# Feed-forward of a routed language-model layer: rows turned three blocks ahead in place of two, with four pairs of buffers for their halves

## What is computed

```python
h = tok(x)                                  # position, nesting and segment tables, einsum with W
h = h + attn(layernorm(h))                  # 8 heads of 64, causal mask, softmax
h = h + ffn(layernorm(h))                   # 8 experts, the best 2 of them per token

# ffn
topk_val, topk_idx = top_k(x @ router_w.T + router_b, 2)
cw = one_hot(topk_idx) * softmax(topk_val)          # weight of each expert
h1, h2 = split(x @ fc1_w[e].T + fc1_b[e], 2)        # 128 -> 2 * 256
y = (silu(h1) * h2) @ fc2_w[e].T + fc2_b[e]         # 256 -> 128
out = sum_e y * cw[e]
```

## Time and profile before

| | |
|---|---|
| time, median of 3 runs | 1257.07 us (1255.15 to 1257.45) |
| the profiled execution's own time | 1256.33 us |
| its span, first to last instruction | 1254.6 us |
| PE busy in the span | 1172.8 us (93%) |
| DVE, ACT, POOL busy | 993.3, 992.7, 755.2 us |
| feed-forward in the span | about 844 us to the end |

### The profile page before, as it was taken

One profiled execution on the slowest core, in us unless ns is written; L12 is line 12 of the kernel. 1 busy time (PEld: TensorE's weight loads), 2 busy tenths in 40 slices (PEclk: granted clock), 3 DMA queues, 4 the chain that ended last, 5 costly groups with the idle time before them and its releaser, 6 DMA issues. The chain is left out here.

```text
span 1254.6 us, 45360 instructions
## 1 busy us (share of the span) xinstructions
PE 1172.8 (93%) x13125; PEld 1031.4 (82%) x13126; DVE 993.3 (79%) x3799; ACT 992.7 (79%) x3491; POOL 755.2 (60%) x1082
## 2 busy tenths in 40 slices
PE   6899999999999999999999999729999997999996
PEld 4578888888888888888888887619999996999995
DVE  6568988888888888888888887756777774777774
ACT  2799999999999999999999998726666664666663
POOL 6436755565565555565565555544777774777775
PEclk9899999999999999999999999968999998999998
DMA  5151110100100111110010111115666663555552
GB/s 177 60 186 56 39 35 32 43 32 32 47 32 32 43 36 32 42 37 32 32 43 32 36 43 40 53 53 170 197 206 199 203 191 130 159 143 143 159 153 68
DMA packets 68049, 108.97 MB, mean 87 GB/s; under 512 B 12756, under 2 KB 32948, under 8 KB 67860
## 3 DMA queue, kind: packets, MB, share of 16 engines
q1 hardware_dynamic: 50068, 62.67, 17.7%
q0 software_dynamic: 17920, 45.55, 10.0%
HBM read 45.66 MB, written 54.11 MB: 80 GB/s over the span
## 5 line engine op out<-in xcount | busy, mean ns | idle before, releaser
L764 ACT ACTIVATE probs<-ps,neg_max 128x128 f32<-128x128 f32 (+1 forms) x1024 | 337.8, 363 | 2.0 <-DVE neg_max L961 1.9
L764 ACT ACTIVATION_READ_ACCUMULATOR probs<-ps,neg_max 128x1 f32 x1024 | 236.3, 231 | 0.0
L574 POOL TENSOR_TENSOR probs<-probs,inv_sums 128x384 f32<-128x384 f32 x120 | 99.2, 826 | 205.4 <-DVE inv_sums L910 205.4
L1143 DVE SCALAR_TENSOR_TENSOR probsT<-ps,b_now,masked 128x256 f32<-128x256 f32 x286 | 125.3, 480 | 85.5 <-PE ps L1237 66.0
L1235 PE MATMUL ps<-xT_hi,w_now 128*128 128x256 f32 x572 | 173.1, 303 | 0.8 <-DVE xT_lo L1127 0.8
L720 ACT ACTIVATE masked<-ps,b_now 128x256 f32<-128x256 f32 x286 | 119.8, 471 | 59.5 <-PE ps L1237 59.1
L1237 PE MATMUL ps<-xT_hi,w_now 128*128 128x256 f32 x572 | 162.8, 285 | 0.0
L1236 PE MATMUL ps<-xT_lo,w_now 128*128 128x256 f32 x572 | 161.9, 283 | 0.0
L631 POOL DMA_INDIRECT xs<-normed,row x128 | 137.0, 1070 | 41.2 <-issue 36.9
L1418 PE MATMUL ps<-w,probsT 128*128 x1144 | 150.8, 275 | 0.0
L1363 PEld LDWEIGHTS ps<-probsT,v 128*64 128x64 f32 x2048 | 109.8, 137 | 45.2 <-issue 44.4
(11 more groups left out here) (243 smaller groups left out, 3181.8 us busy)
## 6 DMA issues: line engine op xcount, KB each, us to landing
v<-xs SPq DMA_DIRECT2D x108, 260.0 KB
kT<-xs SPq DMA_DIRECT2D x35, 260.0 KB
xs<-pad_rows SPq DMA_DIRECT2D x16, 520.0 KB, 3.4
normed<-h SPq DMA_DIRECT2D x32, 256.0 KB, 2.6
w_parts<-in_w SPq DMA_DIRECT2D x1, 2048.0 KB, 8.9
xs<-normed,row POOLq DMA_INDIRECT x128, 2.7
xs<-v POOLq DMA_INDIRECT x108
out_h<-v POOLq DMA_INDIRECT x108
```

Source lines behind the costliest of these rows:

```text
L764: ins = nc.scalar.activation(probs_p[par][:, half, slots[n]], ps[:, SCORES + half, slots[n]], ACT.Exp, bias=neg_max[par][:, half, n:n + 1] ...
L1143: V.scalar_tensor_tensor(actT[z][:, f], ps[:, H2[z], f * BLK:(f + 1) * BLK], b1_now[j % WBUFS][:, 2 + f:3 + f], gate[z][:, f], ALU.add, AL ...
```

## The change

Rows are turned and halved three blocks ahead in place of two, and `x3_hi` and `x3_lo` have four buffers each in place of two. The number 2 in `halve`, `rest`, `rows_in` and the loops before a pass becomes `AHEAD` = 3. The new buffers are second halves of tiles that exist already. The eight buffers `xt`, the two PSUM banks `XB`, the loads, the writes and everything else stay. The core of the diff:

```diff
+AHEAD = 3
...
-        x3_hi = [xT_hi[0][:, 0:BLK], xT_hi[1][:, 0:BLK]]; x3_lo = [xT_lo[0][:, 0:BLK], xT_lo[1][:, 0:BLK]]
+        x3_hi = [t[:, m * BLK:(m + 1) * BLK] for t in xT_hi for m in range(2)]; x3_lo = [t[:, m * BLK:(m + 1) * BLK] for t in xT_lo for m in range(2)]
...
-            def halve(n, z):
+            def halve(n, j):
 
                 act.wait_ge(x3T_full, LEAD + n + 1)
-                act.wait_ge(h2_full, LEAD + n - 1)
-                nc.scalar.copy(x3_hi[z], ps[:, XB[z], 0:BLK]).then_inc(x3hi_ready, 1)
+                act.wait_ge(h2_full, LEAD + n + 1 - len(x3_hi))
+                nc.scalar.copy(x3_hi[j % len(x3_hi)], ps[:, XB[j % 2], 0:BLK]).then_inc(x3hi_ready, 1)
...
                 if not last:
-                    halve(n + 2, z)
+                    halve(n + AHEAD, j + AHEAD)
...
-            def rest(n, z):
-
+            def rest(n, j):
+
+                m = j % len(x3_hi)
                 dve.wait_ge(x3hi_ready, LEAD + n + 1)
-                V.tensor_tensor(x3_lo[z], ps[:, XB[z], 0:BLK], x3_hi[z].bitcast(F32), ALU.subtract).then_inc(x3lo_ready, 1)
+                V.tensor_tensor(x3_lo[m], ps[:, XB[j % 2], 0:BLK], x3_hi[m].bitcast(F32), ALU.subtract).then_inc(x3lo_ready, 1)
...
-                    if not last or n + 2 <= (PH - 1, LAST)[k]:
-                        rest(n + 2, j % 2)
+                    if not last or n + AHEAD <= (PH - 1, LAST)[k]:
+                        rest(n + AHEAD, j + AHEAD)
...
                 if not last:
-                    rows_in(n + 2, i + (j + 2) // XBUFS, (j + 2) % XBUFS)
+                    rows_in(n + AHEAD, i + (j + AHEAD) // XBUFS, (j + AHEAD) % XBUFS)
...
             for k in range(TOPK):
                 pe.wait_ge(table_ready, LEAD + k + 1)
-                for n in range(2):
+                for n in range(AHEAD):
                     rows_in(k * PH + n, k * turns, n)
```

More of the change, by code:

```diff
@@ L829, in _ @@
                 for n in range((k + 1) * PH - XBUFS, min((k + 1) * PH, LAST + 1)):
-                    block_of(n, n % XBUFS, experts, last=(n + 2 > (PH - 1, LAST)[k]), ahead=(n + WBUFS - 1 <= LAST))
+                    block_of(n, n % XBUFS, experts, last=(n + AHEAD > (PH - 1, LAST)[k]), ahead=(n + WBUFS - 1 <= LAST))
         @block.vector
@@ L1405, in fc1 @@
                     ins = three(ps[:, bank[z], f * BLK:(f + 1) * BLK], w1_now[j % WBUFS][:, cols], w1_now[j % WBUFS][:, lows],
-                                x3_hi[z], x3_lo[z])
+                                x3_hi[j % len(x3_hi)], x3_lo[j % len(x3_hi)])
                 ins.then_inc(full, 1)
@@ L1465, in _ @@
                 for n in range((k + 1) * PH - XBUFS, min((k + 1) * PH, LAST + 1)):
-                    block_of((k + 1) * turns - 1, n % XBUFS, last=(n + 2 > (PH - 1, LAST)[k]))
+                    block_of((k + 1) * turns - 1, n % XBUFS, last=(n + AHEAD > (PH - 1, LAST)[k]))
                 e = pe.value_load(table_e[0:1, n:n + 1], min_val=0, max_val=EXPERTS - 1)
```

## The result

The changed kernel takes 1264.81 us (median of five runs, 1262.47 to 1266.46), the kernel before 1257.45 beside it: ratio 1.0063, 95% interval 1.0047 to 1.0079, so 7.4 us slower. Two later comparisons give 1.0044 (1.0027 to 1.0061) and 1.0042 (1.0027 to 1.0057), so 5.6 to 5.9 us. The forecast was +3.4 us, and its range ended at 1264.5; the two later medians, 1262.94 and 1262.58 us, lie inside it, the first does not. The direction was right. The size was not, and the loss did not arise where the sum had put it.

The account below looks back on a forecast made before the run. PE was taken as the bound, 2.65 us a block. Terms 1.8 + 0.5 + 0 + 0.3 + 0.5 + 0.3 gave +3.4 us on 1257.07, so 1260.5 us, range 1257.4 to 1264.5; the forecast's own range was 1258.8 to 1262.5.

Parts of the forecast that it names:

- blocks 13 to 18: Early first pass: PE waits for loads at blocks 13, 14 and 18, whose cover gets thin; +1.8 us.
- blocks 20 to 63: Rest of first pass: several blocks with about 3.1 us of cover against loads of 2.7 to 3.6; +0.5 us.
- start of pass one: Block 2's transposes now stand before block 0's `fc1` and delay every product of the first pass; +0.3 us.
- start of pass two: Block 2's transposes ahead of `fc1`, their load third in flight; +0.5 us, bounds 0 and 0.9.
- pass two and its end: Second pass: output writes move fewer bytes, only block 116's place goes short; +0.3 us (0 to 1.2).
- Blocks 64 to 71: End of first pass: thin covers, but POOL, 2.5 us behind, hides PE's 1.1 us; +0, to +1.1 without that cover.
- Halves one block earlier: ACT's and DVE's halves made one block earlier: gain at most PE's 0.3 us wait, taken as 0.
- Rival A: Loads arrive in time after all; only the starts and some tenths remain, +0.8 to +2.0, 1258.4 us; chance 0.34.
- Rival B: Ring of eight load buffers bounds the first pass, each turn losing 0.3 to 0.5 us; 1264 us; chance 0.21.
- The load's latency: Time a load takes from issue to landing: at least 2.7, 3.6 between the passes, 2.9 us taken.

Follow-up runs that it names:

- r5: The change again, unaltered, against the kernel before: 1262.94 us against 1257.04, ratio 1.0044.
- r17: The change as it stands, once more, against the kernel before: 1262.58 us, ratio 1.0042.
- r14: The change with 32 unused bytes that shift the weight tiles in SBUF, against the unshifted kernel before: 1261.38 us, ratio 1.0032.
- r13: The kernel before with 32 unused bytes that shift the weight tiles in SBUF, against the kernel before: 1254.14 us against 1257.09, ratio 0.9972.

## Why the prediction went wrong in size

The terms of the sum, as the profiles give them, in us. The change, r5 and r17 are set against the kernel before, r14 against r13, which has the same addresses.

| term | predicted | change | r5 | r17 | r14 |
|---|---|---|---|---|---|
| `fc2` of blocks 0 to 24 ("blocks 13 to 18") | +1.8 | 1.3 | 1.0 | 1.7 | 2.8 |
| 24 to 56 ("blocks 20 to 63") | +0.5 | 0.3 | 0.4 | 0.3 | 2.1 |
| 56 to 71, less what is hidden | 0 | 2.2 | 0.6 | 1.3 | 0.6 |
| start of pass one | +0.3 | 0.0 | 0.5 | 0.4 | 0.3 |
| start of pass two | +0.5 | 1.4 | 1.0 | 0.4 | 0.9 |
| pass two and its end | +0.3 | 0.7 | 0.7 | 0.7 | 0.5 |
| feed-forward in all | +3.4 | 5.9 | 4.1 | 4.9 | 7.2 |
| ahead of the first load | 0 | 4.2 | 2.8 | 1.3 | 0.4 |

*Blocks 64 to 71: +0, hidden by POOL's backlog.* This is the step that failed. The prediction saw POOL 2.5 us behind at the end of pass one and took all of it for a cover. Two things were wrong with that. First, the backlog is a cause: POOL's pause at block 56, and the backlog from it, send the loads from block 64 on out late, and with a lead of three PE feels that at once (1.64 us at blocks 64 to 66). Second, of the 2.5 us at the last block only 1.0 could hide anything. Up to block 70 POOL is some 1.1 us behind. The rest arises at the very end in any case: the last two products come 1.2 us apart, and POOL needs 2.53 us for a block.

```profile
1041.33 0.60 DVE L1133 SCALAR_TENSOR_TENSOR kT<-ps,kT 128x128 f32<-128x128 f32 x2
...
1043.91 0.96 POOL L666 DMA_INDIRECT xs<-kT  x1 [0.30 <-issue]
```

These are block 70's in the kernel before: 2.58 us, where 1.42 is usual. In the change POOL had no backlog left before the last block, and waited for PE's work ahead of its writes of blocks 67 and 68:

```profile
1043.73 0.96 POOL L667 DMA_INDIRECT xs<-v  x1 [1.71 <-DVE v L1135]
...
1046.88 0.96 POOL L667 DMA_INDIRECT xs<-v  x1 [0.93 <-DVE v L1135]
```

At the last block it is still 1.5 us behind. From `fc2` of block 71 to the first load of pass two it is 6.75 us before and 5.79 after, so 0.96 were hidden. PE lost 3.2 us between blocks 56 and 71, which leaves 2.2; some 1.7 of the 3.2 come with block 70's load of 5.87 us and the block behind it, of which the rows before show nothing. Where the slow transfer cost less, the term is 0.6 (r5). The bound of +1.1 that the prediction gave came from block 70 alone, with no look at what blocks 64 and 65 would lose first. They were not in the rows that it read.

*Blocks 13 to 18: +1.8.* The size came out about right, but not for the reason given. The thin covers of blocks 14 and 18 hung on the writes of blocks 6 and 10, from which it was 6.1 and 5.9 us to the next load. A packet of queue 8 is in flight at 877.7 and another at 887.2 us, as with block 70 above. In the five profiles of the change it is 3.7 to 4.5. In the change's own profile PE turns blocks 13, 14 and 15 without a wait:

```profile
884.20 0.38 PE L1398 MATMUL ps<-ident,v 128*128 128x128 f32 x2
886.84 0.38 PE L1398 MATMUL ps<-ident,kT 128*128 128x128 f32 x2
889.49 0.38 PE L1398 MATMUL ps<-ident,kT 128*128 128x128 f32 x2
```

What it lost up to block 24 is 0.2 us each behind the transposes of blocks 9 and 16 and 0.4 each behind those of 18 and 26, at the boundaries of the loop. So the sign that the prediction named, PE waiting for loads first at blocks 13 to 18, did not show: the first wait of weight is at block 64. Only r14 has one at block 14 (1.12 us). That the sum of this term is near is luck.

*Blocks 20 to 63: +0.5.* Between blocks 24 and 56 0.3 to 0.5 us, and 2.1 in r14, whose block is shorter. Right for the kernel as it stood.

*Halves one block earlier: 0.* Right. PE had 0.3 us of such waits and has none; four pairs with a lead of two make no difference (0.9999, on a slow chip).

*Starts: +0.3 and +0.5.* The second is up to 1.4, over its bound of 0.9. The third load was the right thing to look at: it held `fc1` back by 0.3 to 0.7 us. What the granted clock adds or takes at either start is as large, and differs from run to run.

*Pass two: +0.3.* Between `fc2` of blocks 72 and 142 +0.4, and as much again behind it. What the prediction did not have is that it is POOL's second pause, at block 106, that makes blocks 114 to 116 short.

*The stage ahead* stood in the sum at nothing, since the change does not touch it. It holds 4.2 us of the 10.1 between the first pair of spans, and 1.3 of 6.2 in r17's. The medians differ by 7.4 and 5.6, since single executions of the change scatter by some 3 us to either side. Where these microseconds come from stays open.

*The range.* The upper ends of the terms add up to 2.5 + 1.5 + 1.1 + 0.9 + 0.9 + 1.2 = 8.1 us, so 1265.2, and not to the 1262.5 that the prediction gave for them.

*Rival A* (the loads arrive in time) was right that the late landings behind blocks 14 and 18 need not come again, and wrong that little would then be left: 4.1 us at least. *Rival B* (the ring becomes the bound) had the right size for another reason: losses don't return in every turn, as the turns from 24 to 56 show, but come where POOL, a write or a load is late. A lead of four is where B holds. The 1.9 us of room that the prediction worked out for the ring at a lead of three were 1.3 by the usual times of write and load. That is enough in the steady part, and a pause of 1.65 us above the usual uses it up.

*The load's latency:* 2.9 taken; the profile of lead four gives 2.8 as the median from issue to landing (2.5 to 4.0), and block 70's 5.87 shows how far one can stand out. The Trainium skill ("DMA: Bandwidth & Descriptors", section "Anatomy of one DMA — SWDGE (gpsimd) path") gives 2.6 by its fit, an estimate. The fit is for DMAs that GpSimd issues, and these loads are SP's, so it is no more than a neighbour's figure. By it the sum would have been smaller still, and the measurement decides.

## What to carry to other kernels

Work ahead by one more step is not free when the buffers that feed it stay the same: what counts is buffers minus lead, and the next step off can cost ten times as much (+6 us, then +66). The loss can be worked out beforehand: divide the fixed part of the round trip (9.3 us here) by the buffers less the lead less one, and compare with a block's time. Do it with the usual times, then ask how much of the room one late write or one pause takes. An engine that is behind is cover for the one that it waits for only by the backlog that it brings along, and only if nothing else hangs on it; here POOL's writes free the buffers that PE's next loads need, so the same backlog has to be entered as a cost first. A thin cover read from one execution may be chance: look at a second trace before building a term on it. And a control with the same addresses belongs beside any experiment that changes a table's size: here 32 bytes were worth 3 us.

## What was not expected of the hardware

- The place of the weights in SBUF changes how closely TensorE's fp32r matmuls of 128 x 256 follow each other: 0.118 us with `w1_now0` at byte 201280, 0.114 with it 32 bytes further on, along with the other shifted tiles. Only these two places were tried, and no run shows a rule. The kernel before with nothing but that shift takes 1254.14 us (0.9972), less than the change and less than the kernel before. Twelve buffers with a lead of two, at the same addresses, take 1253.46 and are not to be told from it. The Trainium skill's page "SBUF — State Buffer", section "Operand start alignment", speaks of such addresses as a matter of legality and says that its runs timed nothing; these did.
- POOL stands still for 1.95 us between the two writes of block 56 and again of block 106, in the profiles of the kernel before, the change (all of them on the faster chips) and lead four; with twelve buffers and either lead it is 1.8 us, at blocks 56 and 102. What it does there the profile does not say.
- On two chips of the same kind the same program takes 11 to 12% longer, some nine tenths of it in the feed-forward, where ACT and DVE wait two to three us for results of PE again and again. The change costs 0.4 to 0.6% on one sort and 1.1 to 1.2% on the other. On the first the loads are what PE waits for; on the second it waits for the gated product.
